# Attention: scores in three single banks with exponentials of 128x512, and a ring of row maxima of four banks instead of three

## What is computed

```python
def proj(W, b):
    return (x @ W.T + b).reshape(B, S, H, hd).transpose(0, 2, 1, 3)
Q, K, V = (proj(Wq, bq), proj(Wk, bk), proj(Wv, bv))
scale = 1.0 / jnp.sqrt(jnp.float32(hd))
scores = jnp.einsum('bhqd,bhkd->bhqk', Q, K) * scale
attn = jax.nn.softmax(scores, axis=-1)
out = jnp.einsum('bhqk,bhkd->bhqd', attn, V)
...
```

## Time and profile before

| what | value |
|---|---|
| median of three runs | 2127.63 us |
| the profiled execution's own time | 2127.73 us |
| its span, first to last instruction | 2125.9 us |
| TensorE busy | 1809.8 us (85% of the span) |
| VectorE busy | 1201.9 us (57%) |
| ScalarE busy | 905.9 us (43%) |
| attention, first to last matmul of its own | 113 to 907 us of the span |

### The profile page before, as it was taken

One profiled execution on the slowest core, in us unless ns is written; L12 is line 12 of the kernel. 1 busy time (PEld: TensorE's weight loads), 2 busy tenths in 40 slices (PEclk: granted clock), 3 DMA queues, 4 the chain that ended last, 5 costly groups with the idle time before them and its releaser, 6 DMA issues. The chain is left out here.

```text
span 2125.9 us, 37885 instructions
## 1 busy us (share of the span) xinstructions
PE 1809.8 (85%) x11264; PEld 1147.6 (54%) x11265; DVE 1201.9 (57%) x2635; ACT 905.9 (43%) x1362; POOL 436.5 (21%) x570
## 2 busy tenths in 40 slices
PE   7889999999999999976599999999994885067771
PEld 4423444444444444363488888888884465036551
DVE  4578888888888888644611111111113896946334
ACT  3436666666666666743033223323331520031333
POOL 2210000000000000030033333333331001202772
PEclk9969999999999999997799999999997998575996
DMA  4511111111111111054343433444442001141224
GB/s 146 187 42 35 31 34 33 30 37 30 33 34 30 37 30 32 14 166 169 138 109 95 114 113 100 107 116 112 97 112 81 1 1 60 64 158 23 48 40 161
DMA packets 103320, 159.38 MB, mean 75 GB/s; under 512 B 20704, under 2 KB 79392, under 8 KB 97760
## 3 DMA queue, kind: packets, MB, share of 16 engines
q1 hardware_dynamic: 69712, 118.46, 17.3%
q0 software_dynamic: 22656, 24.51, 6.7%
q10 hardware_dynamic: 10896, 15.73, 2.2%
HBM read 124.19 MB, written 49.02 MB: 81 GB/s over the span
## 5 line engine op out<-in xcount | busy, mean ns | idle before, releaser
L548 DVE TENSOR_REDUCE unit_max<-ps_ring 128x1 f32<-128x512 f32 x1024 | 639.6, 684 | 70.5 <-PE ps_ring L423 64.4
L534 ACT ACTIVATE w<-ps_scores 128x1024 f32<-128x1024 f32 x512 | 503.6, 1022 | 265.4 <-PE ps_scores L500 262.7
L423 PE MATMUL ps_ring<-k_stack,q_stack 96*128 96x512 bf16 x1024 | 367.5, 393 | 21.1 <-POOL v_padded L386 9.5
L500 PE MATMUL ps_scores<-q_stack,k_stack 98*128 98x512 bf16 x1024 | 307.3, 382 | 2.6 <-ACT w L534 2.5
L1513 PE MATMUL m_ps_h<-m_xt,m_w 128*128 128x256 f32 x1248 | 278.5, 382 | 0.8 <-DVE m_xt L1564 0.8
L1525 PE MATMUL m_ps_y<-w,m_ht 128*128 x1248 | 275.8, 379 | 0.0
L445 PE MATMUL ps_o<-w,v_padded 128*32 128x256 f32 x4096 | 260.8, 384 | 0.0
L1513 PEld LDWEIGHTS m_ps_h<-m_xt,m_w 128*128 128x128 f32 x1248 | 238.9, 192 | 34.1 <-DVE m_xt L1564 1.2
L1525 PEld LDWEIGHTS m_ps_y<-w,m_ht 128*128 128x128 f32 x1248 | 234.2, 190 | 30.3
L423 PEld LDWEIGHTS ps_ring<-k_stack,q_stack 96*128 96x128 bf16 x1024 | 98.7, 97 | 262.0 <-DVE unit_max L548 177.1
L1545 ACT ACTIVATE m_ht<-m_ps_h,m_w 128x256 f32<-128x256 f32 x312 | 130.7, 470 | 144.6 <-PE m_ps_h L1513 144.6
(11 more groups left out here) (244 smaller groups left out, 1860.4 us busy)
## 6 DMA issues: line engine op xcount, KB each, us to landing
m_w<-in_w SPq DMA_DIRECT2D x39, 1028.0 KB, 4.9
rows<-g_rows SPq DMA_DIRECT2D x16, 512.0 KB, 2.9
y<-sums SPq DMA_DIRECT2D x16, 512.0 KB, 7.6
q_parts<-qk_part SPq DMA_DIRECT2D x16, 384.0 KB, 3.7
k_parts<-qk_part SPq DMA_DIRECT2D x16, 384.0 KB, 3.8
q_stack<-q_parts SPq DMA_DIRECT2D x64, 96.0 KB
k_stack<-k_parts SPq DMA_DIRECT2D x64, 96.0 KB
xt<-in_xt ACTq DMA_DIRECT2D x8, 512.0 KB, 4.3
```

What stands on the lines that cost most here:

```text
L423: nc.tensor.matmul(out[:, :], qs[0:STACK, u, qt * P:(qt + 1) * P], ks[0:STACK, u, half * HALF:(half + 1) * HALF], start=True, stop=True).t ...
L500: mm = nc.tensor.matmul(p_s[kt % 2][:, half * HALF:(half + 1) * HALF], ks[:, u, kt * P:(kt + 1) * P], qs[:, u, half * HALF:(half + 1) * HALF],
L534: nc.scalar.activation(pt[:, kt, :], p_s[kt % 2][:, :], ACT.Exp, scale=SCALE)\
L548: nc.vector.tensor_reduce(unit_max[:, u % 2, half, qt:qt + 1], src[:, :], axis=AX.X, op=ALU.max).then_inc(ring_used, 1)
```

## The change

The scores get three banks of 128x512 (`p_s` of three tiles, one bank each) instead of two pairs. Each score matmul is now a unit of its own, numbered `h = 2 * kt + half`, 0 to 15 in a head. It goes to bank `SCORE_BANK[h]`, waits for the exponential that last read this bank, and each exponential covers 128x512 and waits for its one matmul. `score_gap` gives how many units back the same bank was used. The bank freed goes to the ring, `RING = 4`.

```diff
-RING = 3
+RING = 4
...
-        p_s = [mem.ps(f"ps_scores{u}", (P, S)) for u in range(2)]
+        p_s = [mem.ps(f"ps_scores{u}") for u in range(3)]
+        SCORE_BANK = (0, 1, 2) * 5 + (1,)
...
+        def score_gap(h):
+
+            return next(d for d in range(1, 2 * KT) if SCORE_BANK[(h - d) % (2 * KT)] == SCORE_BANK[h])
...
-                            wait_from(sp, scores_ready, (g * SLOTS + u) * KT)
+                            wait_from(sp, scores_ready, (g * SLOTS + u) * 2 * KT)
...
-                    pe.wait_ge(exp_done, n * KT + EDGES[i + 1])
+                    pe.wait_ge(exp_done, n * 2 * KT + 2 * EDGES[i + 1])
...
-                            wait_from(pe, exp_done, n * KT + kt - 1)
                             for half in range(2):
-                                mm = nc.tensor.matmul(p_s[kt % 2][:, half * HALF:(half + 1) * HALF],
-                                                      ks[:, u, kt * P:(kt + 1) * P],
-                                                      qs[:, u, half * HALF:(half + 1) * HALF],
-                                                      start=True, stop=True)
-                            mm.then_inc(scores_ready, 1)
+                                h = 2 * kt + half
+                                wait_from(pe, exp_done, n * 2 * KT + h - score_gap(h) + 1)
+                                nc.tensor.matmul(p_s[SCORE_BANK[h]][:, :], ks[:, u, kt * P:(kt + 1) * P],
+                                                 qs[:, u, half * HALF:(half + 1) * HALF],
+                                                 start=True, stop=True).then_inc(scores_ready, 1)
...
-                            act.wait_ge(scores_ready, n * KT + kt + 1)
                             if kt in EDGES:
 
                                 wait_from(act, pv_done, (n - 1) * BURSTS + EDGES.index(kt) + 1)
-                            nc.scalar.activation(pt[:, kt, :], p_s[kt % 2][:, :], ACT.Exp, scale=SCALE)\
-                                .then_inc(exp_done, 1)
+                            for half in range(2):
+                                h = 2 * kt + half
+                                act.wait_ge(scores_ready, n * 2 * KT + h + 1)
+                                nc.scalar.activation(pt[:, kt, half * HALF:(half + 1) * HALF], p_s[SCORE_BANK[h]][:, :],
+                                                     ACT.Exp, scale=SCALE).then_inc(exp_done, 1)
```

## The result

The changed kernel took 2133.09 us, the kernel before 2124.40 (medians of 20 runs each), ratio 1.0041 with a 95% interval of 1.0031 to 1.0051: 8.7 us slower, where 8.4 were forecast. The 2136 us that the forecast names lies 3 us above the 2133, because it started from the median of three runs, 2127.63, and over 20 runs the kernel before has 2124.40. A few executions took far longer than the rest (9367 us one of the kernel before, 2786 and 6453 us two of those beside e5 to e7, 7216 us one of e7), and the ratios, and the median given for e7, leave them out. In the profiled executions the span went from 2125.9 to 2132.5 us.

A forecast was written before the change was run, and what follows sets the result against it. TensorE sets the pace at 12.12 us per head, 0.54 of it waiting for the ring. -0.54 + 0.61 + 0.03 gives +0.10 per head, +6.0 over 60 heads; with the ends +8.4 on 2127.73: 2136 us, range 2129 to 2144.

The forecast's parts named there:

- The sum: Per head -0.54 + 0.61 + 0.03 = +0.10 us, +6.0 over heads 2 to 61; with start and ends +8.4 us.
- The wait of unit 15: In kt 7 the last score matmul waits for the exponential of h = 13: 0.61 us per head, new.
- the chain of 2.57 us: From unit 10's start to unit 15's: 0.41 + 1.50 + 0.60 + 0.06 us, against 1.96 unhindered.
- the second wait: Where kt is 3 or 6, a second wait before the exponential makes that step 0.52 instead of 0.49 us.
- The three hundredths for units 3 and 13 and the late weights: 0.01 us each on units 3 and 13 and on the matmul behind unit 15: 0.03 us per head.
- The ring's waits: TensorE's waits for normalisation and reductions, 0.54 us per head, all to go with the fourth ring bank.
- the fifth ring matmul behind a fold: With four ring banks it still loses about 0.13 us to a reduction, swallowed by the wait of unit 15.
- The edges of the stage: Heads 0 and 1 +1.0 us, the start up to 133 us -0.6, the last two heads +2.0.
- rival 2: Balance: exponential step at its lower bound, units 3 and 13 free; about +0.01 us per head, 2130 us; chance 0.22.
- Rival 3: A dearer chain: units 3 and 13 wait too or steps reach 0.52; +0.1 us per head, 2142 to 2145; chance 0.14.
- rival 1: Faster: halved exponentials free banks sooner, unit 15 hardly waits, chain under about 2.43 us; 2123, without wait 2096; chance 0.09.
- rival 4: Waits of 0.6 us drop TensorE's clock from 1.00 to 0.50 in a tenth of heads: +12, 2148 us; chance 0.04.

The follow-up runs named there:

- e5: The changed kernel with the bank table of e1 and RING = 3, one bank of PSUM unused: 2124.76 us, ratio 1.0006 to the kernel before.
- e7: The changed kernel with the table of e1 and, in heads without a fold, kt 7's second maxima matmul between the two scores: 2098.65 us, ratio 0.9879.
- e1: The changed kernel with another SCORE_BANK table, short reuses at h = 5 and 10 behind a PV burst instead of 15 and 1: 2099.12 us, ratio 0.9901.
- e3: The changed kernel with four single score banks in turn and RING = 3, so the halved exponentials alone: 2121.16 us, ratio 0.9994 to the kernel before.
- e2: The changed kernel with RING = 3, its own bank table kept, one bank of PSUM unused: 2144.99 us, ratio 1.0110 to the kernel before.

## Why the prediction was right

- **The sum.** Forecast +0.10 us per head and +8.4 in all; measured +0.108 and +8.7. The likeliest case came true, and by its own mechanism. That the sum fits so well is partly luck: the cost was put about 0.05 us too high and the ring's gain as much too high, as the next two points show. With only the first of them put right, the forecast would have been about +0.05 us per head, with only the second about +0.16.
- **The wait of unit 15.** Forecast 0.61 us, measured 0.58. Of the chain of 2.57 us the start of 0.41 measured 0.42 and the three steps of together 1.50 measured 1.46; what is left of the 2.54 for the last exponential and the release is 0.66, as forecast. The 0.03 us put on the second wait, where `kt` is 6, did not appear. The three hundredths for units 3 and 13 and the late weights were nearly nothing: units 12 and 13 start 0.22 us apart (0.60 at 523.84). That puts the cost about 0.05 too high. The forecast also said 0.8 us between the two scores "in every head". Behind a fold they start 0.65 us apart, since there the 0.15 us of ring wait stays in front of them (the prediction itself had worked out 0.13); what is the same in both kinds of head is the 2.54 us from unit 10.
- **The ring's waits.** Forecast 0.54 us per head. e5 against e1 gives 0.38, but e1 has 0.05 of unit 15's wait and some 0.05 of the fifth ring matmul behind a fold; with these the removed waits come to 0.48. The changed kernel gives the same: the cost of 0.58 to 0.59 less the 0.108 by which the head grew. The excess of 0.06 probably lies in the small terms of the sum over a pair (0.07 for late scores, 0.05 for slower folds), but no run takes these singly.
- **The edges of the stage.** In the last head `kt` 5 to 7 were to take 2.88 us instead of 2.25:

```profile
911.59 0.82 PE L506 MATMUL ps_scores<-q_stack,k_stack 98*128 98x512 bf16 x3
912.67 0.88 PE L506 MATMUL ps_scores<-q_stack,k_stack 98*128 98x512 bf16 x2 [0.26 <-ACT w L540]
914.13 0.39 PE L506 MATMUL ps_scores<-q_stack,k_stack 98*128 98x512 bf16 x1 [0.59 <-ACT w L540]
914.45 2.37 PE L450 MATMUL ps_o<-w,v_padded 128*32 128x256 f32 x40
```

They take 914.45 - 911.59 = 2.86. The stretch from 141.5 to 150 us, first before and then after, shows a term that the forecast did not have:

```profile
141.50:150.00 8.50, 8.50 (x84) 3.42 (x80) 6.84 (x12) 5.33 (x6) 0.85 (x4) 0.98 0.18 48
```
```profile
141.50:150.00 8.50, 8.08 (x67) 2.92 (x59) 5.19 (x10) 3.80 (x8) 0.85 (x4) 0.85 0.10 25
```

The granted clock averaged 0.85 there instead of 0.98: it rose from 0.50 (1.2 GHz) to 1.00 (2.4 GHz) two microseconds later. From the first matmul of attention to this rise it is 28.6 us in the one and 30.3 in the other, and between 22.9 and 31.0 in the seven experiments, so it is not put down to the change. Attention as a whole, first to last matmul of its own, took 10.2 us longer in these two executions and the rest of the program 3.6 us less. Of the 10.2 us 6.5 lie between the first and the last of the 61 transposes, 1.0 before and 2.7 behind: the ends cost 3.7 us here where the forecast had 2.4. But single executions of the kernel before spread over more than 10 us, and only the medians are to be trusted to a microsecond or two.
- **The rivals.** On the side of the cost the measured 0.58 to 0.59 us lies between rival 2's 0.55 and the forecast's 0.64, for its step (0.48) and its free units 3 and 13 were nearly right; its sum fails because it kept 0.54 us for the ring's gain, where 0.48 was measured. Rival 3 had the wrong direction. The halves don't help by themselves (e3: 0.9994), so rival 1 had no footing; what made its sign come true in e1 is the place of the reuse. The chain was 2.54 us, not under 2.43. The clock stayed at 1.00 from 150 us on with standstills of up to 0.58 us in each head: rival 4 did not happen. What the page TensorE: Matmul & The Clock Gate of the Trainium skill describes in its section A second HAM failure mode: psum-queue depth-cycling does not show here. By the page ScalarE: Activation LUTs of the Trainium skill, section What ACT_TABLE_LOAD costs, the estimates were 0.61 and 0.52 us for one exponential of this shape and its step; the rows have 0.603 in the mean and 0.485, so the measured step decides and is the smaller.

## What to carry to other kernels

When a ring of buffers is walked by a number of units that it doesn't divide, some unit looks back one place less. In this kernel it waited where the consumer had just been refilled and worked without a pause (0.58 us at h = 15, 0.47 at h = 9). Put that unit right behind a stretch in which the producer is busy with something else: here the table of banks alone, with no other difference, separates 2133 us from 2099 (ratios 1.0041 and 0.9901, so about 30 us). And when two waits guard one engine, removing one is worth only what the other doesn't take. Measure them crossed, as e2, the changed kernel, e5 and e1 do: the fourth ring bank is worth 0.23 us per head beside the short reuse at h = 15 and 0.38 without it, and the short reuse costs 0.33 us with three ring banks and 0.48 with four.

## What the runs showed of the hardware

Halving an exponential of 128x1024 cost ScalarE little: 1022 ns became 603 in the mean, but back to back the step went from 0.92 to 0.485 us, so two halves take 0.97 us where the whole took 0.92. ScalarE's busy time from 150 to 885 us rose from 501.46 us to 526.00. In e3 it is 531.50, and the ratio of 0.9994 shows that this by itself costs nothing here. Three banks for the scores did what four did (e5, 1.0006), though the kernel before had been using both pairs. And a wait of TensorE is partly hidden in its timeline, by the 0.16 us for which two records of 128x512 normally overlap: 0.58 us of standstill reads as 0.42 of idle time.
